# Products of zeros on TensorE between the second mixture and the feature attention's second unit

## The reference, cut to what matters

```python
def _L3_xattn_ref(q, k, v):
    ...
    h = N_HEAD                       # 8
    qh = q.reshape(b * h, d // h, m)
    kh = k.reshape(b * h, d // h, -1)
    vh = v.reshape(b * h, c // h, -1)
    scale = 1.0 / jnp.sqrt(jnp.asarray(d // h, dtype=q.dtype))
    qk = jnp.einsum('bdm,bdn->bmn', qh, kh) * scale
    sm = jax.nn.softmax(qk, axis=-1)
    ret = jnp.einsum('bmn,bcn->bcm', sm, vh)
...
x = x + _L2_ffn_ref(_layernorm(x), ...)   # the second mixture
x = x + _L3_xattn_ref(_layernorm(x), ctx_2048, ctx_2048)
x = x + _L3_ffn_ref(_layernorm(x), ...)
```

## Time and profile before

| | us |
|---|---|
| median of 3 runs | 1070.21 |
| the runs | 1069.6 to 1072.03 |
| the profiled execution, its own time | 1070.49 |
| its span, first to last instruction | 1068.7 |
| PE busy over the span | 980.7 (92%) |
| DVE busy over the span | 526.0 (49%) |
| mean granted clock of TensorE | 0.952 |

### The profile page before, as it was taken

The page is one execution under the profiler, slowest core; times in us unless marked ns, Lnnn a source line. Parts: engine busy times, 40 slices in busy tenths (PEclk is TensorE's granted clock), DMA queues, the critical chain, the costliest instruction groups (busy, mean ns, idle before and its releaser), DMA issues.

```text
span 1068.7 us, 18450 instructions
## 1 busy us (share of the span) xinstructions
PE 980.7 (92%) x7228; PEld 693.9 (65%) x7228; DVE 526.0 (49%) x1264; ACT 322.0 (30%) x620; POOL 233.8 (22%) x322
## 2 busy tenths in 40 slices
PE   5979999989999999969775899999959999999999
PEld 4866699446766667658654799999823434353477
DVE  7877323445435344465376121212158787748541
ACT  4852133232122221214310211111114566743100
POOL 5421441500000000012520222222162443400000
PEclk9996999999999999989985999999967999999999
DMA  9103132210101010035002765666321300020000
GB/s 284 50 12 99 30 100 84 84 50 31 36 19 40 26 41 11 6 117 187 2 27 82 288 240 204 229 220 224 131 65 36 151 1 1 1 80 0 1 15 25
DMA packets 39996, 88.95 MB, mean 83 GB/s; under 512 B 4712, under 2 KB 27592, under 8 KB 36584
## 3 DMA queue, kind: packets, MB, share of 16 engines
q1 hardware_dynamic: 32520, 73.60, 20.1%
q0 software_dynamic: 4080, 11.15, 3.7%
q10 hardware_dynamic: 3312, 3.02, 0.8%
HBM read 76.35 MB, written 11.40 MB: 82 GB/s over the span
## 4 chain that ended last, share of the span: by engine, by line
PE 78%; DVE 12%; ACT 3%; issue 2%; DMA 2%; POOL 2%; DVEq 0%; ACTq 0%; POOLq 0%
PE bank L358 23%; PE bank L1323 11%; PE bank L1342 7%; PE bank L1667 6%; PE bank L2389 5%; PE bank L2414 3%; PE bank L2435 3%; PE bank L2859 3%; PE bank L1313 3%; PE bank L1678 2%; PE bank L1643 2%; PE bank L2453 1%; PE bank L2865 1%; DMA big<-yg,big 1%; DVE big L2244 1%
## 5 line engine op out<-in xcount | busy, mean ns | idle before, releaser
L358 PE MATMUL bank<-XNT,big 128*128 128x512 f32 x296 | 135.0, 605 | 2.9 <-DVE big L2620 1.5
L1323 PE MATMUL bank<-big 128*128 128x128 f32 x1012 | 118.5, 277 | 0.1
L1323 PEld LDWEIGHTS bank<-big 128*128 128x128 f32 x1012 | 116.5, 194 | 0.6 <-issue 0.5
L2389 PE MATMUL bank<-big,xs 32*128 32x512 f32 x256 | 88.8, 732 | 12.1 <-DVE xs L285 10.4
L358 PEld LDWEIGHTS bank<-XNT,big 128*128 128x128 f32 x296 | 54.8, 192 | 64.7 <-issue 59.5
L274 POOL TENSOR_TENSOR rstd<-ve,half 128x1 f32<-128x1 f32 x48 | 27.9, 584 | 301.1 <-DVE ve L268 300.9
L2244 DVE TENSOR_REDUCE big<-bank 128x2 f32<-128x512 f32 x128 | 82.0, 685 | 20.2 <-PE bank L2389 19.5
L1342 PE MATMUL bank<-big 128*128 (+1 forms) x368 | 87.2, 380 | 1.1 <-DVE big L1108 0.7
L1101 DVE TENSOR_TENSOR big<-big,bank 128x640 f32<-128x640 f32 x23 | 18.9, 822 | 136.6 <-ACT big L1211 136.6
L2335 ACT ACTIVATE big<-bank 128x1024 f32<-128x1024 f32 x64 | 64.9, 1025 | 39.2 <-PE bank L2414 38.9
L1342 PEld LDWEIGHTS bank<-big 128*128 128x128 f32 (+1 forms) x368 | 66.3, 190 | 9.0 <-issue 1.9
(11 more groups left out here) (358 smaller groups left out, 1638.7 us busy)
## 6 DMA issues: line engine op xcount, KB each, us to landing
big<-m_gu SPq DMA_DIRECT2D x23, 1408.0 KB, 6.1
big<-m_d SPq DMA_DIRECT2D x8, 768.0 KB
big<-a_qk SPq DMA_DIRECT2D x16, 256.0 KB, 2.8
yg<-big ACTq DMA_DIRECT2D x23, 128.0 KB, 2.1
big<-m_gu SPq DMA_DIRECT2D x8, 352.0 KB
big<-a_o SPq DMA_DIRECT2D x16, 128.0 KB, 2.0
xn<-XNT SPq DMA_DIRECT2D x8, 256.0 KB, 2.1
big<-f_keys SPq DMA_DIRECT2D x1, 2048.0 KB, 10.9
```

The costliest lines, as they stand in the source:

```text
L358: ins = e.matmul(out, a, b, start=start and n == 0, stop=stop and n == len(pairs) - 1)
L1323: ins = e.matmul(gu[:, n if n <= WHOLE else n + 1], gu_slot[s % SLOTS][:, c:c + P], xgT[s % 2][:, kb, :], start=kb == 0, stop=kb == KB - 1)
L2389: e.matmul(bank[:, step_bank(step), :], k.xs[t % 2][q, b * P:(b + 1) * P], cm[t % 2][q, 2 * jp:2 * jp + 2].rearrange("p j n -> p (j n)"), ...
```

## The change

A helper `zeros(n)` in the feature attention's PE program issues n products of the 128x128 tile of zeros with itself into the first 128 columns of bank 7. That bank is written afresh by the first values, so no result changes. It is called in four places: 44 products ahead of the first score, 10 ahead of `turn_maxima(0)` (and so behind the sixteenth score), 6 behind the scores of unit 4, and 2 behind each of the eight scores that PE makes in unit 0 of the loop. That is 76 products. No other engine's program is touched, and no wait is added or taken away.

```diff
+        def zeros(n):
+
+            for _ in range(n):
+                e.matmul(bank[:, VB, 0:P], k.zeros[:, :], k.zeros[:, :], start=True, stop=True)
+
         e.sem_inc(k.xt_ps, NT)
         after(e, "ld", 16)
+        zeros(44)
         for u in range(FRONT):
             for r in range(RG):
                 scores(u, r)
             if u == UNITS - 1:
+                zeros(10)
                 turn_maxima(0)
+        zeros(6)
         for u in range(NU):
...
             for n, r in ahead[2 * (u > 0):]:
                 scores(n, r)
+                if u == 0:
+                    zeros(2)
```

## The result

The changed kernel takes 1076.48 us (median of 6 runs, 1075.4 to 1078.85), beside 1071.81 us for the kernel before in 6 runs (1069.6 to 1073.14): a ratio of 1.0048, 95% interval 1.0037 to 1.0059. By the ratio that is 5.1 us slower (1071.81 x 0.0048); the forecast was 3.4. (Its 1073.6 us was counted on the three runs then known, whose median lies 1.6 us lower.) The profiled execution took 1076.27 us.

A forecast was written before the change was run, and what follows sets the result against it. PE, busy 92% of the span, was at half clock in part of this stretch. 2.04 us to unit 0's `turned` plus 2.9 for the pairs minus 1.58 gave 3.4 slower: 1070.21 + 3.4 = 1073.6 us, range 1068 to 1079.

The forecast's parts named there:

- zeros(44) hidden: Ahead of the first score: 44 zeros take 9.8 us, 773.5 to 783.3, hidden by the layernorm until 783.74 with 0.4 us to spare.
- The first top 0.94 us sooner, and DVE's run with it: First maximum after 1.13 us instead of 2.07; DVE's gapless run ends at 795.33 instead of 796.27.
- The clock falls among the lone scores and half of the ten zeros' time is lost: After step 15: clock falls between 788 and 792.5, seven of ten zeros run at half clock, `turn_maxima(0)` 0.83 us later.
- 4.7 us on to `turned`: From `turn_maxima(0)` to unit 0's `turned`, six zeros included: 4.7 us, so `turned` at 801.85, 2.04 us later.
- 14.35 us for `turned` and eight scores with pairs: Unit 0's `turned` to unit 1's: 1.07 plus eight scores with two zeros each at 1.66; 14.35 us against 11.46, 2.9 more.
- the break-even of 1.24: Scores of units 5 and 6: below 1.24 us for a score with its pair, the faster rival would decide.
- 1.58 us back at the end: From unit 1's `turned`, 811.27 to 814.48: 3.21 us becomes 1.63 at full clock, a gain of 1.58.
- The clock that holds: Rival, chance 0.18: full clock from 773 us on, `turn_maxima(0)` at 795.33; 1.5 us slower, 1071.7.
- the rule beside it: Skill's advice to leave no idle gaps between matmul bursts; by it the changed kernel would not lose its clock.
- Zeros hidden beside scores: Rival, chance 0.14 wholly or in part: zeros run beside scores on other row groups, DVE binds; 5.4 us faster, 1064.8.
- A second fall: Rival, chance 0.09: clock falls again among scores with zeros, some 1.4 us more a step, 7 to 8 us on top, 1081.
- Zeros that do not hold the clock: Rival, chance 0.04: clock falls at 776.9 as before, the 44 last until 789.2, later fillers at half clock; 1080 or more.

## Why the prediction was right, point by point

- *zeros(44) hidden.* Right. They took from 772.76 to 782.8, and the first score still waited for the layernorm; alone they changed nothing (ratio 1.0000).
- *The first top 0.94 us sooner, and DVE's run with it.* Half right, and the one step that the mechanism had wrong: the top came 1.15 us after the first score (1.13 forecast), but `norm(1)` gave all of it back, ending behind GpSimd's L2174, a wait that the forecast did not have. The rows held a hint of it: `norm(1)` took 0.77 us where `norm(0)` took 0.42. This is shown: with GpSimd's order changed it took 0.40 us. It put step 15 at 8.33 us behind the first score (792.45) instead of the 7.36 of the forecast: 0.97 us of the error.
- *The clock falls among the lone scores and half of the ten zeros' time is lost.* Right in kind (789.9). Seven of the ten were taken at half clock, and in the profiled execution all ten were: 4.43 us instead of 3.95, 0.48 more. When the clock comes back differs: without the pairs and with four zeros, which are the same kernel up to there, it came back among the ten, and they took 3.86 and 3.56 us. With the step before it `turn_maxima(0)` came 2.28 us later than before, not 0.83.
- *4.7 us on to `turned`.* 5.39, as the scores of steps 16 to 18 too began at half clock; in the two profiles just named it was 4.80. The zeros' share was as forecast: 1.53 us for six (1.49).
- *14.35 us for `turned` and eight scores with pairs.* 14.41. The step is 1.69 us (1.66 forecast, bounds 1.51 and 1.71), and the break-even of 1.24 was far off. The doubled pairs show the same price once more.
- *1.58 us back at the end.* 1.57 (818.68 to 820.32 is 1.64).
- *The rivals.* The clock that holds, to which the rule beside it pointed (the Trainium skill, TensorE: Matmul & The Clock Gate, "Why this matters for your kernels"), did not happen: in all profiles without zeros among the lone scores the clock fell there, without the 44 behind nearly gapless records and with them behind a wait of 1.1 us for the tops that `norm(1)` had put off. Zeros hidden beside scores: refuted by steps of 1.69 and 2.14 us. A second fall: not in the changed kernel, but without the ten and six the half clock did last through the pairs (3.16 us a step). Zeros that do not hold the clock: refuted; from 773.2 to 784.1 PE made little but zeros, and the clock was 1.00.

The forecast's range held the time; its likeliest value was 2 us low on the execution's own sum (5.56 against 3.4), nearly all of it ahead of unit 0's `turned`: 0.97 us at `norm(1)`, 0.48 in the ten zeros and 0.69 from `turn_maxima(0)` on. The first stands in every profile that has the 44 and GpSimd's old order; the other two hang on the moment at which the clock comes back. No error was made up by another, so the range was not met by luck.

## What to carry to other kernels

A product put in to keep the clock costs its full price wherever it parts products that would run side by side on other row groups; ask of each place what PE would have waited for, and put the fillers in blocks there. Giving one engine its speed back pays only as far as the next one can use it: here DVE was held by GpSimd's work, which half-speed scores had hidden, and only both changes together gave 0.4%. And the longest idle gap need not be the one to fill: the 44 zeros of 76 bought nothing.

## What the runs showed of the hardware that was not expected

DVE's `norm` (a tensor-scalar from SBUF to SBUF) and its three-operand additions did not end before a GpSimd tensor product that had begun before or with them, and took 1.73 and 2.17 us where, with no GpSimd work beside them, they take 0.40 and 0.48. DVE's reductions out of PSUM were not held: in the kernel before, the one at 801.89 took 0.69 us inside L2174's 800.94 to 802.84, as one by itself does. Where an addition began first (without the pairs, 803.59 before 803.92), it took 0.66 us, and GpSimd's L2174 was the longer one, 2.08 us instead of 1.90. The Trainium skill (SBUF — State Buffer, "Who interferes with whom") says that a DVE instruction with two SBUF inputs contends with a GpSimd instruction that reads SBUF, that a tensor-scalar can enter modes in which the two contend for a shared pair of ports and whoever issues first blocks the other for the whole instruction, and that reductions do not contend on this chip. These traces agree in who waits and until when; the ports themselves no run here shows.

TensorE's clock did not follow the share of time in which PE has records: in the kernel before it fell at 790.6 under lone scores of 32 rows whose records covered 3.24 of 3.40 us, and without the ten and six zeros it stayed at half for 23.6 us of gapless scores and pairs, while in the changed kernel the same pairs, begun at the full clock, kept it.
